# Scatters, staged parts, softmax and the output weight's pieces at new places in a hand-ordered attention step

## The chip, the cores and the metric

The kernel runs on one core of one Trainium2 chip. The metric is device microseconds of one execution. Engines are named as the profile names them: PE is TensorE (matmuls), DVE is VectorE, ACT is ScalarE, POOL is GpSimd, SP is SyncE, which here only issues DMAs.

## The reference, cut to what matters

x is 8 x 2048 x 512 in float32 (8 batches). Six modulation rows per batch (`sa, ca, ga, sb, cb, gb`) come from a small matmul.

```
h = layernorm(x) * (1 + ca) + sa
xn = layernorm(h) * gamma + beta
k, v, r = xn @ Wk.T, xn @ Wv.T, xn @ Wr.T
csum = cumsum(k * v * sigmoid(td) ** t) over the 2048 tokens
wkv = sigmoid(tf) * k * v + sigmoid(td) * (csum shifted by one token)
x = x + ga * ((sigmoid(r) * wkv) @ Wo.T)
h = layernorm(x) * (1 + cb) + sb
x = x + gb * (moe_0(h) + moe_1(h)) / 2     # each: 32 experts, top 2 of a softmax, SwiGLU, 512-256-512
```

## The kernel before, in words

There are two stages. The first, which the change touches, does everything up to the second norm, the router and the lists of tokens for each expert; the second works through the experts' tiles of 128 tokens. Matmuls are made in three passes of float32r: every operand is kept as a high part (a cast, made by ACT) and a low part (the difference, made by POOL or DVE).

The first stage is 32 **steps**, 4 for each batch, of 512 tokens. Batch 0 is written out, batches 1 to 7 are a hardware loop whose body is four steps (s = 0 to 3). Each engine's program has a function `step(b, s, first)` in which its work stands in a fixed order written by hand; semaphores tie the engines together. Work of several steps is in flight: in step s, PE projects step s (`project`, four chunks of 128 output channels, each k, v and r), multiplies Wo for step s-1 (`output`, between chunks 0 and 1), counts ranks for step s-2, transposes the second norm's result of step s-1 (`back`, inside chunk 3), transposes the first norm's result of step s+1 (`front`), and makes the router's logits of step s-1 (`logits`, last).

The names that the text uses:

- DVE: `chunk(dc)` (L829 to L844) turns k, v into the weighted cumulative sum in `cs` (the scan, L841) and `aa`. `topk` (from L894), `place` (L923 to L942, which ends with the scatter indices `sidx`), `residual` (L852, L856), `modulate` (L872, L877, which makes `h2`), and four parts of `norm_front`: statistics of x two steps ahead (part 0, L778), `hb` (part 1, L793), `hb` again with the second set of statistics (part 2, L799), and the small `nmg` (part 3, L815). `split_x` (L822) makes the low part of the transposed input.
- ACT: `chunk_k` (L553), `chunk_r` (L559), `hi(dc)` (L565, the high part `sTh`), `soften` (L583, L585: the softmax's exponentials, with a table load before it and another at the next sigmoid), `turned` (L595), `logits` (L602, the copy of the logits to `lgt`), `normed` (L608), `front` (L616).
- POOL: `receive(dc)` (L678, multiplies by the sigmoid), `lo(dc)` (L701, the low part `sTl`), three `rstd` (L672), `scatter` (L711: 16 indirect DMAs per step put token numbers and weights into the experts' lists).
- The **staged parts**. The experts' weights are split into high and low parts on the way: a step has 10 jobs (40 per batch, of which 4 are the pieces of Wo, which are also scaled by `ga` on POOL in `scale_wo`). Job j is: SP loads 256 KB into `sraw[j % 4]` (`stage_in`), ACT casts it to `shigh[j % 2]` (`stage_hi(j)`, L576), POOL or DVE makes the low part in place (`stage_lo(j)`, L693 or L886), SP stores both halves (`stage_out(j)`, L357, 512 KB). So `stage_hi(j)` waits until job j-2 has been stored. `DVE_LOW` says which jobs of a step have their low part on DVE.
- SP's order in a step is ten turns; turn i stores job i-1, then loads job i+2. After turn 4 stands the 1 MB store of x (`store_x1`), after turn 5 the 1 MB store of `h2` (`store_h2`), after turn 0 the 1 MB load of x. Even turns up to 6 also issue a 256 KB store of a modulation row.

PSUM's 8 banks are handed round: group q of step s lies in bank (26 s + q) mod 8, and PE waits for the reader of the group 8 earlier. So `back` waits for the scan of chunk 1, and the second of `front`'s four groups waits for the scan of chunk 3 (both L841).

## Time and profile before

| | |
|---|---|
| time before, median of 3 runs | 5015.96 us (5013.2 to 5016.27) |
| time of the profiled execution | 5032.62 us, span 5030.9 us |
| PE, DVE, ACT, POOL busy | 92%, 60%, 33%, 56% of the span |
| first stage, steps | from about 80 us to about 2010 us |
| second stage, expert tiles | from about 2120 us to the end |

Busy shares are of the whole span. PE's busy time counts overlapped matmuls and is no measure of how fast it runs; the granted clock (1.00 is 2.4 GHz, 0.50 is 1.2 GHz) stands beside it in the tables of stretches.

### The profile page before, as it was taken

Reading aid. Unit: us, or ns where it says so; the run is one execution under the profiler, and the core shown is the slowest. Engines: PE = TensorE matmul, PEld = TensorE weight load, DVE = VectorE, ACT = ScalarE, POOL = GpSimd, SP = SyncE. Lnnn points to the kernel's source line nnn. Section 1 sums busy time; section 2 is a strip of 40 time slices with the busy share of each in tenths; the row PEclk is TensorE's granted clock in tenths of the full one; section 3 lists DMA queues with packets and bytes.
Section 4 is the critical chain, followed back from the end, with each engine's and each line's share of the span. In section 5 each row is a group of like instructions: output and inputs, shape, how many; then the busy total and the mean of one; then the engine's idle time right before and its main releaser. Section 6 shows DMA issues by size and latency. Waiting matters only on the chain.

```text
span 5030.9 us, 89180 instructions
## 1 busy us (share of the span) xinstructions
PE 4643.5 (92%) x22649; PEld 3825.1 (76%) x22649; DVE 3011.9 (60%) x6077; ACT 1635.8 (33%) x4093; POOL 2804.4 (56%) x2303
## 2 busy tenths in 40 slices
PE   6999999989988999499989998999999999999998
PEld 4777777777777777377777776888788888888886
DVE  5888888888888888444444443554344444444443
ACT  2344444444444444122222222332222222222222
POOL 2576666666666666544454544555455555555554
PEclk8999999999999999799999999999999999999999
DMA  6666565656665656589999989999999989998897
GB/s 234 214 198 212 181 199 181 207 185 213 186 208 185 207 183 199 204 248 277 274 276 268 272 265 271 266 278 248 282 237 245 236 230 253 241 240 215 220 230 192
DMA packets 434624, 1152.46 MB, mean 229 GB/s; under 512 B 59361, under 2 KB 59362, under 8 KB 415666
## 3 DMA queue, kind: packets, MB, share of 16 engines
q0 software_dynamic: 182512, 454.27, 38.8%
q1 hardware_dynamic: 231106, 619.79, 36.2%
q10 hardware_dynamic: 20736, 75.51, 4.0%
q8 instruction: 83, 1.36, 0.1%
q14 instruction: 187, 1.53, 0.1%
HBM read 719.35 MB, written 463.57 MB: 235 GB/s over the span
## 4 chain that ended last, share of the span: by engine, by line
PE 39%; DMA 13%; issue 4%; POOL 2%; DVE 1%; POOLq 0%; SPq 0%; DVEq 0%; ACT 0%
DMA out<-c_yo,c_idx 12%; PE ps L1322 11%; PE ps L1324 11%; PE ps L1323 11%; PE ps L1331 4%; PE ps L1350 2%; DMA c_wt<-wsp_d 1%; POOL out L1313 1%; POOL c_xg L1280 1%; POOLq L1305 0%; DVE c_yo L1577 0%; POOL list_d L1285 0%; DMA list_d<-pairs,sidx 0%; DMA c_lists<-list_d,c_rowu 0%; DVE c_xl L1565 0%
## 5 line engine op out<-in xcount | busy, mean ns | idle before, releaser
L1313 POOL DMA_INDIRECT out<-c_yo,c_idx x576 | 919.0, 1595 | 922.0 <-DMA out<-c_yo,c_idx 481.4
L1322 PE MATMUL ps<-c_wt,c_xh 128*128 128x512 f32 x2304 | 964.7, 419 | 27.6 <-issue 20.3
L1324 PE MATMUL ps<-c_wt,c_xl 128*128 128x512 f32 x2304 | 911.0, 395 | 0.0
L1323 PE MATMUL ps<-c_wt,c_xh 128*128 128x512 f32 x2304 | 904.9, 393 | 0.0
L1280 POOL DMA_INDIRECT c_xg<-h2g_d,c_idx x576 | 566.9, 984 | 512.2 <-DVE c_yo L1577 406.8
L1561 DVE TENSOR_TENSOR c_hh<-ps,c_sil 128x256 f32<-128x256 f32 x576 | 244.1, 424 | 926.1 <-ACT c_sil L1404 926.0
L1577 DVE SCALAR_TENSOR_TENSOR c_yo<-ps,c_wc,c_xg 128x512 f32<-128x512 f32 x576 | 432.4, 751 | 521.2 <-PE ps L1324 265.9
L444 PE MATMUL ps<-xTh,wTh 128*128 128x512 f32 x1536 | 640.1, 417 | 46.9 <-DVE cs L841 34.8
L1409 ACT CAST c_xh<-ps 128x512 fp32r<-128x512 f32 x576 | 337.1, 585 | 957.5 <-PE ps L1331 956.1
L445 PE MATMUL ps<-xTl,wTh 128*128 128x512 f32 x1536 | 627.0, 408 | 0.0
L446 PE MATMUL ps<-xTh,wTl 128*128 128x512 f32 x1536 | 625.4, 407 | 0.0
L711 POOL DMA_INDIRECT list_d<-pairs,sidx x496 | 523.6, 1056 | 177.2 <-issue 120.8
L1404 ACT ACTIVATE c_sil<-ps 128x256 f32<-128x256 f32 x576 | 221.2, 384 | 1181.5 <-PE ps L1324 1181.5
L1322 PE MATMUL ps<-c_wt,c_hTh 128*128 128x512 f32 x1152 | 456.9, 397 | 71.3 <-DVE c_hTl L1570 71.3
L1322 PEld LDWEIGHTS ps<-c_wt,c_xh 128*128 128x128 f32 x2304 | 437.1, 190 | 104.7 <-issue 30.8
L1324 PEld LDWEIGHTS ps<-c_wt,c_xl 128*128 128x128 f32 x2304 | 435.6, 189 | 105.1
L1323 PEld LDWEIGHTS ps<-c_wt,c_xh 128*128 128x128 f32 x2304 | 439.2, 191 | 77.9
L1565 DVE TENSOR_TENSOR c_xl<-ps,c_xh 128x512 fp32r<-128x512 f32 x576 | 397.4, 690 | 132.6 <-ACT c_xh L1409 132.1
L1324 PE MATMUL ps<-c_wt,c_hTl 128*128 128x512 f32 x1152 | 454.9, 395 | 0.0
L1323 PE MATMUL ps<-c_wt,c_hTh 128*128 128x512 f32 x1152 | 452.9, 393 | 0.0
L444 PEld LDWEIGHTS ps<-xTh,wTh 128*128 128x128 f32 x1536 | 307.8, 200 | 125.0 <-DVE cs L841 47.9
L446 PEld LDWEIGHTS ps<-xTh,wTl 128*128 128x128 f32 x1536 | 305.7, 199 | 67.9
(202 smaller groups left out, 7767.7 us busy)
## 6 DMA issues: line engine op xcount, KB each, us to landing
c_wt<-wsp_d SPq DMA_DIRECT2D x69, 2048.0 KB, 11.4
sraw<-wex SPq DMA_DIRECT2D x290, 256.0 KB, 3.5
wsp_d<-shigh SPq DMA_DIRECT2D x288, 256.0 KB
wsp_d<-sraw SPq DMA_DIRECT2D x288, 256.0 KB
c_wt<-wsp_d SPq DMA_DIRECT2D x69, 1024.0 KB, 12.5
xin<-x SPq DMA_DIRECT2D x34, 1024.0 KB, 7.9
h2g_d<-mod_d SPq DMA_DIRECT2D x128, 256.0 KB, 6.2
out<-xin SPq DMA_DIRECT2D x32, 1024.0 KB, 6.7
```

The costliest lines, as they stand in the source:

```text
L444: nc.tensor.matmul(o, lh, rh, start=first, stop=False)
L445: nc.tensor.matmul(o, lh, rl, start=False, stop=False)
L446: return nc.tensor.matmul(o, ll, rh, start=False, stop=last)
L711: nc.gpsimd.indirect_dma_start(out=list_d, out_offset=bass.IndirectOffsetOnAxis(ap=sidx[:, s % 2, i:i + 1], axis=0), in_=pairs[:, s % 2, i ...
L1280: nc.gpsimd.indirect_dma_start(out=xg[:, n % RING, :], out_offset=None, in_=h2g_d, in_offset=bass.IndirectOffsetOnAxis(ap=idx[:, n:n + 1], ...
L1313: nc.gpsimd.indirect_dma_start(out=out, out_offset=bass.IndirectOffsetOnAxis(ap=idx[:, n:n + 1], axis=0), in_=yo[:, n % 4, :], in_offset=N ...
L1322: nc.tensor.matmul(o, lh, rh, start=first, stop=False)
L1323: nc.tensor.matmul(o, lh, rl, start=False, stop=False)
L1324: return nc.tensor.matmul(o, ll, rh, start=False, stop=last)
L1409: nc.scalar.copy(xh[:, s % 2].rearrange("p k t -> p (k t)"), ps[:, 4 + s % 2, :]).then_inc(x_hi, 1)
L1565: V.tensor_tensor(xl[:, s % 2].rearrange("p k t -> p (k t)"), ps[:, 4 + s % 2, :], xh[:, s % 2].rearrange("p k t -> p (k t)").bitcast(F32) ...
L1577: V.scalar_tensor_tensor(out=yo[:, s % 4, :], in0=ps[:, 6 + s % 2, :], scalar=wc[:, s % 4:s % 4 + 1], in1=xg[:, s % RING, C:2 * C], op0=AL ...
```

## The change

The change touches only the first stage. The same instructions are issued in another order, and nothing is left out.

- Wo's pieces are jobs 5 to 8 of a batch in place of 2 to 5; `scale_wo` stands in POOL's step by name.
- The low parts on DVE are jobs 1, 5 and 8 of each step in place of 4, 5 and 6; POOL has 0, 2, 3, 4, 6, 7 and 9.
- ACT: the cast of the next step's job 0 stands at the end of a step, ahead of the copy of the logits; `soften` stands ahead of `chunk_r(0)`; `hi(0)` behind the casts of jobs 2 and 3; the casts of jobs 7 and 8 ahead of `chunk_k(3)`.
- POOL: three scatters stand first in the step, three more after job 0, eight after the third `rstd` as before; `lo(0)` is later; jobs 6 and 7 stand between the eight scatters and `receive(1)`.
- DVE: `topk` is first in the step; job 1's low part follows chunk 0; between `modulate` and chunk 1 only job 5's low part is left; job 8's low part stands between chunk 2 and the statistics of `norm_front` part 0, which stay ahead of chunk 3.
- SP's wait in `stage_out` becomes a `gate` (the same wait, with one for the value 1 ahead of it when the count is in a register).

```diff
-DVE_LOW = (4, 5, 6)
-WO_PART = {2: 0, 3: 1, 4: 2, 5: 3}
+DVE_LOW = (1, 5, 8)
+WO_PART = {5: 0, 6: 1, 7: 2, 8: 3}
...
             def stage_out(b, j):
-                wait(sp, low_of(j), lows(b, j))
+                gate(sp, (low_of(j), lows(b, j)))
...
             def step(b, s, first):          # ACT
-                stage_hi(b, at)
+                if first and s == 0:
+                    stage_hi(b, 0)
                 stage_hi(b, at + 1)
                 chunk_k(b, s, 0)
-                chunk_r(b, s, 0)
-                hi(b, s, 0)
                 if not (first and s < 2):
                     soften(b, s - 2)
+                chunk_r(b, s, 0)
...
             def step(b, s, first):          # DVE
+                if not (first and s < 2):
+                    topk(b, s - 2)
                 norm_front(b, s + 1, 1)
                 chunk(b, s, 0)
-                if not (first and s < 2):
-                    topk(b, s - 2)
+                stage_lo(b, s * PER_STEP + 1)
                 norm_front(b, s + 1, 2)
...
                     place(b, s - 2)
-                stage_lo(b, s * PER_STEP + 4)
                 if not (first and s == 0):
                     modulate(b, s - 1)
                 stage_lo(b, s * PER_STEP + 5)
-                stage_lo(b, s * PER_STEP + 6)
                 chunk(b, s, 1)
                 chunk(b, s, 2)
+                stage_lo(b, s * PER_STEP + 8)
                 norm_front(b, s + 2, 0)
                 chunk(b, s, 3)
```

What now stands where, on two engines. POOL in step 3 of batch 0, from the third `rstd` (`rsb`) on; `sg` is `receive`, `sTl` is `lo`, `sraw<-sraw,shigh` is a job's low part. Before:

```order
L672 TENSOR_TENSOR rsb<-vab,half 128x4
L711 DMA list_d<-pairs,sidx 1048704x2 x8
L678 TENSOR_TENSOR sg<-sg,aa 128x512
L711 DMA list_d<-pairs,sidx 1048704x2
L701 TENSOR_TENSOR sTl<-sg,sTh 128x512
L678 TENSOR_TENSOR sg<-sg,aa 128x512
L693 TENSOR_TENSOR sraw<-sraw,shigh 128x512
```

POOL at the same place of the changed kernel:

```order
L676 TENSOR_TENSOR rsb<-vab,half 128x4
L712 DMA list_d<-pairs,sidx 1048704x2 x8
L697 TENSOR_TENSOR sraw<-sraw,shigh 128x512 x2
L682 TENSOR_TENSOR sg<-sg,aa 128x512
L712 DMA list_d<-pairs,sidx 1048704x2
L702 TENSOR_TENSOR sTl<-sg,sTh 128x512
L682 TENSOR_TENSOR sg<-sg,aa 128x512
```

The low parts of jobs 6 and 7 have moved in between the eight scatters and the multiplication of chunk 1.

ACT in step 3 of batch 0, from `chunk_k(1)` (the first `aa`) on; `sg` is `chunk_r`, `sTh` is `hi`, `h2T` is `turned`, `shigh<-sraw` a job's cast. Before:

```order
L553 ACTIVATE aa<-ps,bias 128x512
L576 CAST shigh<-sraw 128x512
L559 ACT_TABLE_LOAD
L559 ACTIVATE sg<-ps,bias 128x512
L553 ACTIVATE aa<-ps,bias 128x512
L565 CAST sTh<-sg 128x512
L595 COPY h2T<-ps 128x512 x4
L559 ACTIVATE sg<-ps,bias 128x512
L553 ACTIVATE aa<-ps,bias 128x512
L565 CAST sTh<-sg 128x512
L576 CAST shigh<-sraw 128x512 x2
```

ACT at the same place of the changed kernel:

```order
L553 ACTIVATE aa<-ps,bias 128x512
L559 ACTIVATE sg<-ps,bias 128x512
L576 CAST shigh<-sraw 128x512
L553 ACTIVATE aa<-ps,bias 128x512
L576 CAST shigh<-sraw 128x512
L559 ACTIVATE sg<-ps,bias 128x512
L565 CAST sTh<-sg 128x512
L576 CAST shigh<-sraw 128x512
L553 ACTIVATE aa<-ps,bias 128x512
L595 COPY h2T<-ps 128x512 x4
L565 CAST sTh<-sg 128x512
```

The casts of jobs 7 and 8 now stand ahead of the third and fourth `chunk_k` and around `hi(1)`; they stood behind both.

## Rows read from the trace of the kernel before

**Rows 1.** The table of stretches: 29 whole steps of the first stage

The columns are the stretch, its length, then busy time and (count) of PE, PE's weight loads, DVE, ACT, POOL, then PE's granted clock, the DMA share and GB/s.

```profile
187.68:1955.61 1767.93, 1614.04 (x7833) 1334.11 (x7832) 1485.33 (x3248) 735.03 (x1565) 1174.19 (x1008) 0.92 0.63 196
```

**Rows 2.** The waits, 300 to 1900 us: total us, times, longest us

```profile
PE ps L466 <- DVE cs L841: 104.6, 26, 5.3
...
DVE sraw L886 <- ACT shigh L576: 56.0, 19, 3.9
DVE ps L829 <- PE ps L446: 53.4, 25, 6.1
...
DVE nmg L815 <- POOL rsg L672: 46.3, 24, 3.8
```

**Rows 3.** The timeline of PE: start us, duration us, what, [idle before <-releaser]

```profile
187.68 0.48 PE L444 MATMUL ps<-xTh,wTh 128*128 128x512 f32 x1
...
1143.28 2.82 PE L466 MATMUL ps<-ident,h 128*128 128x128 f32 x12 [4.03 <-DVE cs L841]
...
1156.33 3.68 PE L476 MATMUL ps<-rws,h2T 128*128 128x64 f32 x32
...
1955.61 0.48 PE L444 MATMUL ps<-xTh,wTh 128*128 128x512 f32 x1
```

**Rows 4.** The table of stretches: PE's granted clock after two of its waits

```profile
1147.00:1151.00 4.00, 4.00 (x10) 3.13 (x11) 3.39 (x10) 3.12 (x6) 2.11 (x2) 0.50 0.30 84
...
1022.00:1026.00 4.00, 3.82 (x17) 3.17 (x18) 3.93 (x12) 3.11 (x7) 2.48 (x2) 1.00 0.53 140
```

**Rows 5.** The timeline of DVE in one step, and its statistics and scan in another

```profile
1108.27 0.76 DVE L829 SCALAR_TENSOR_TENSOR ps<-ps,bias,aa 128x512 f32<-128x512 f32 x1 [1.88 <-ACT aa L553]
...
1111.85 0.83 DVE L894 MAX8 m<-lgt 128x8 f32<-128x32 f32 x8
...
1115.59 2.73 DVE L799 SCALAR_TENSOR_TENSOR hb<-hb,rsf,mod 128x512 f32<-128x512 f32 x4
...
1121.10 0.68 DVE L852 TENSOR_TENSOR xin<-ps,xin 128x512 f32<-128x512 f32 x1
...
1126.86 1.23 DVE L815 SCALAR_TENSOR_TENSOR nmg<-mvg,rsg 128x4 f32<-128x4 f32 x1
...
1130.52 0.68 DVE L886 TENSOR_TENSOR sraw<-sraw,shigh 128x512 fp32r<-128x512 f32 x1
1131.12 2.73 DVE L872 SCALAR_TENSOR_TENSOR h<-xin,mvb,mod 128x512 f32<-128x512 f32 x4
...
1022.83 2.46 DVE L778 BATCH_NORM_STATS2 stf<-xin 128x6 f32<-128x512 f32 x4
...
1027.29 1.28 DVE L841 TENSOR_TENSOR_SCAN cs<-ones,cs,ps 128x512 f32<-128x512 f32 x1
```

**Rows 6.** The timeline of DVE and POOL at the start of a step

```profile
1158.67 6.13 DVE L793 SCALAR_TENSOR_TENSOR hb<-xin,mvf,mod 128x512 f32<-128x512 f32 x4
...
1161.02 3.24 POOL L693 TENSOR_TENSOR sraw<-sraw,shigh 128x512 fp32r<-128x512 f32 x2 [0.17 <-ACT shigh L576]
```

**Rows 7.** The timeline of SP: issues of the h2 store and of job 9's load

```profile
1136.73 0.39 SPq L331 DMA_DIRECT2D h2g_d<-h  x1
...
1147.47 0.36 SPq L370 DMA_DIRECT2D sraw<-wex  x1
```

**Rows 8.** The timeline of POOL: first of eight scatters, then receive(1)

```profile
1131.37 1.41 POOL L711 DMA_INDIRECT list_d<-pairs,sidx  x1 [2.34 <-DVE sidx L942]
...
1144.10 1.27 POOL L678 TENSOR_TENSOR sg<-sg,aa 128x512 f32<-128x512 f32 x1 [2.37 <-DVE aa L844]
```

**Rows 9.** The timeline of ACT: soften behind hi(0), and the copy of the logits

```profile
1119.33 0.62 ACT L565 CAST sTh<-sg 128x512 fp32r<-128x512 f32 x1 [10.60 <-PE ps L446]
1119.97 1.28 ACT L583 ACT_TABLE_LOAD   x1
...
1123.82 1.13 ACT L576 CAST shigh<-sraw 128x512 fp32r<-128x512 f32 x2
...
1160.05 0.37 ACT L602 COPY lgt<-ps 128x256 f32<-128x256 f32 x1 [1.03 <-PE ps L476]
```

More of the change, by code:

```diff
@@ L633, in step @@
                 chunk_k(b, s, 1)
+                chunk_r(b, s, 1)
                 stage_hi(b, at + 6)
-                chunk_r(b, s, 1)
                 chunk_k(b, s, 2)
+                stage_hi(b, at + 7)
+                chunk_r(b, s, 2)
                 hi(b, s, 1)
+                stage_hi(b, at + 8)
+                chunk_k(b, s, 3)
                 if back_too:
                     turned(b, s)
-                chunk_r(b, s, 2)
-                chunk_k(b, s, 3)
                 hi(b, s, 2)
-                stage_hi(b, at + 7)
-                stage_hi(b, at + 8)
-                front(b, s, (0, 1))
+                stage_hi(b, at + 9)
                 chunk_r(b, s, 3)
-                front(b, s, (2, 3))
+                front(b, s, range(KC))
                 hi(b, s, 3)
+                if s < 3:
+                    stage_hi(b, at + 10)
+                else:
+                    stage_hi(b + 1, 0)
                 if back_too:
                     logits(b, s)
-                stage_hi(b, at + 9)
             normed(0, -1)
@@ L693, in stage_lo @@
                 nc.gpsimd.tensor_tensor(dst, sraw[:, j % 4], high.bitcast(F32), ALU.subtract).then_inc(low_pool, 1)
-                for i in (j + 1,) if j < 3 else (j + 1, j + 2):
-                    if i in WO_PART:
-                        scale_wo(b, i)
             def lo(b, s, dc):
@@ L716, in step @@
                 old = not (first and s < 2)
+                older = not (first and s < 3)
                 at = s * PER_STEP
+                if older:
+                    scatter(b, s - 3, 10, 13)
+                rstd(f_var, vaf, h_ready, rsf, f_rstd, b, s + 1)
                 stage_lo(b, at)
-                if not (first and s < 3):
-                    scatter(b, s - 3, 11, 13)
-                rstd(f_var, vaf, h_ready, rsf, f_rstd, b, s + 1)
-                stage_lo(b, at + 1)
+                if older:
+                    scatter(b, s - 3, 13, 16)
                 receive(b, s, 0)
-                if not (first and s < 3):
-                    scatter(b, s - 3, 13, 14)
-                lo(b, s, 0)
-                if not (first and s < 3):
-                    scatter(b, s - 3, 14, 16)
                 stage_lo(b, at + 2)
@@ L731, in step @@
                 stage_lo(b, at + 3)
+                lo(b, s, 0)
+                stage_lo(b, at + 4)
                 if not (first and s == 0):
                     rstd(b_var, vab, h2_ready, rsb, b_rstd, b, s - 1)
+                if s == 0:
+                    scale_wo(b, 5)
+                    scale_wo(b, 6)
                 if old:
                     scatter(b, s - 2, 0, 8)
+                if s == 0:
+                    scale_wo(b, 7)
+                stage_lo(b, at + 6)
+                if s == 0:
+                    scale_wo(b, 8)
+                stage_lo(b, at + 7)
                 receive(b, s, 1)
@@ L792, in norm_front @@
                     for j in range(TJ):
[L793 to L794 removed]
+                        V.scalar_tensor_tensor(out=hb[:, j, :], in0=xin[:, u, j, :],
+                                               scalar=mvf[:, j, 0:1], in1=mod[:, CA1, :],
+                                               op0=ALU.subtract, op1=ALU.mult).then_inc(h_half, 1)
                 elif part == 2:
```

19 lines of the change are left out of this document (7 added, 12 removed).

## The prediction

> **What bounds the kernel now.** I read the table of stretches first. Over 29 whole steps of the first stage [rows 1] PE's granted clock is 0.92, DVE is busy for 1485.33 of 1767.93 us, and 1767.93 / 29 = 60.96 us is the length of a step. DVE's own work is 1485.33 / 29 = 51.2 us of it. The second stage is untouched, so all that can change is the 60.96, some 30 times (32 steps, of which the first two have no scatters).
>
> The waits come next [rows 2]. In each of 26 steps PE stands 104.6 / 26 = 4.0 us ahead of `back` until DVE has made the scan of chunk 1. DVE is late there because of its own waits: 56.0 / 26 = 2.2 us a step for the cast of a staged part (job 6), ahead of chunk 1; 1.8 us for `rstd`, ahead of `nmg`; and 2.1 us for PE, which had been late from its own stall. So a loop from DVE to PE and back sets the step, and a stall of PE costs more than its length: after the 4.03 us wait at 1143 us [rows 3] the stretch 1147 to 1151 us still runs at 0.50, the 1.2 GHz level [rows 4]; after another wait of such length the second of these stretches is already at 1.00, 2.4 GHz. What follows the wait (12 transposes in 2.82 us [rows 3]) runs at the low level.
>
> The timeline of DVE gives the price of each piece, taken from start to start [rows 5]: chunk 0 3.58 us, `topk` 3.74, `norm_front` part 2 5.51, `residual` 5.76, `nmg` with `place` 3.66 (of which 1.23 is `nmg`, four elements a lane, so mostly a wait in disguise), one low part 0.60, the four instructions of half of `modulate` 2.73; from the statistics of part 0 to the end of the next scan 1027.29 + 1.28 - 1022.83 = 5.74.
>
> **What the change removes.** `topk` moves into the time in which DVE waited for chunk 0 (1.88 us in [rows 5]). Job 6's low part and its 2.2 us of waiting leave the place ahead of chunk 1, and job 4's leaves too; job 1's low part comes in. `soften` used to stand behind `hi(0)`, which waits 10.60 us for the end of `output` [rows 9]; behind it came the casts and low part that POOL's `rstd` for `nmg` was queued behind. From its table load to the next cast it is 1123.82 - 1119.97 = 3.85 us of ACT, now spent while PE runs chunk 0 and the Wo matmuls, so I cost it at nothing: its cover is the ten us and more until `residual`. By DVE's pieces the scan of chunk 1 now ends at about 36 us after the logits, before PE reaches `back`; the stall of 4.0 us there goes. `scale_wo` and SP's extra wait for 1 add instructions of no length that matters beside waits.
>
> **What is late next.** The price is on ACT, POOL and SP. On ACT the cast of job 8 now stands behind the cast of job 7 and behind `hi(1)`; DVE's low part of job 8 waits for it, and behind it are queued the statistics and chunk 3, whose scan releases `front` on PE. On POOL the low parts of jobs 6 and 7 stand ahead of `receive(1)`, on which `hi(1)` waits. And the cast of job 7 waits until job 5 has been stored, which SP issues behind the 1 MB store of `h2`. I work this loop out from the end of PE's logits (time 0):
>
> - logits copied 0.4 [rows 9], `topk` from 0.5 to 4.2, `norm_front` part 1 to 7.2 (2.73 plus 0.3), chunk 0 to 10.8, job 1's low part 11.4
> - `norm_front` part 2: 5.51, plus 1.5 for a clash with POOL (below), to 18.4; `residual` to 24.2; `nmg` and `place` 3.2 (3.66 less half of what `nmg` waited) to 27.4
> - `modulate` up to SP's issue of the `h2` store: 1136.73 - 1131.12 = 5.6 us [rows 5, 7], at 33.0
> - job 5 stored: before, SP's load of job 9, which waits for just that, came 1147.47 - 1136.73 = 10.7 us after the `h2` store [rows 7]. Then job 6's store and a store of x shortly ahead shared the DMA engines; now job 6's store comes later and the store of x, due at the end of `residual` (24.2), has 9 us to drain. I take 7.5 (choice, between 5.4, where POOL would be last, and 10.7), at 40.5
> - cast of job 7 0.7 (half of 1.13 for two [rows 9], and a hand-over), low part 7 on POOL 1.4, `receive(1)` 1.3 (1.27 [rows 8]), `hi(1)` 0.7, cast of job 8 0.5, low part 8 on DVE 0.7 plus 0.3: at 46.1
> - statistics and chunk 3 up to its scan 5.74, at 51.9
> - PE has then stood some 5 us, so the 12 remaining transposes of `front` take 2.8 and the logits 3.68 plus 1.0 (between 0, if the clock is back, and 3, if it is not): 59.5
>
> POOL's own path is shorter: eight scatters from the end of `place` take 1144.10 - 2.37 - 1131.37 = 10.4 us [rows 8], and the low part of job 6 ends at 39.1, ahead of job 7's cast. In the steps with Wo's pieces two scalings of 1.3 us stand on this path, but no store is waited for, and the end is within 1 us of the same. What each engine loses at the loop's edge fell on DVE's path; now DVE waits for the logits in that time. I leave this gain out as a margin.
>
> The sum: 60.96 - 59.5 = 1.5 us a step, times 30 is 44 us. The profiled execution took 5032.62 us with a span of 5030.9, 17 us above the median of 5015.96; the difference is taken off the median: 4972 us.
>
> **The clash with POOL.** Four instructions of L793 took 6.13 us [rows 6] where four of the same shape took 2.73 [rows 5], and POOL's two low parts beside them took 3.24 us, not two times 1.27. Both sides read only SBUF. Before, part 2 of `norm_front` met no POOL arithmetic; now `receive(0)` and job 2's low part fall beside it, two instructions of 1.3 us, so the bounds are 0 and 2.6, and with the larger share falling on DVE I take 1.5. Part 1 instead meets mainly scatters, and gains what L793 lost. The Trainium skill says in SBUF — State Buffer, section Who interferes with whom, that a VectorE instruction with two SBUF inputs contends with a GpSimd instruction that reads SBUF, and that the later one blocks fully. By that rule, the trace agrees at L793, and the clash would come at the upper bound of 2.6; by the rows alone 1.5 stands.
>
> **The rivals.**
>
> *The stall moves and grows (slower).* If job 5's store takes the old 10.7 us after the `h2` store, all behind it is 3.2 later: 62.7 us a step, 1.8 more than before, 53 us: 5069. It decides at 9.0 us: below that the kernel is faster, above it slower. For it: the only row that shows this store is 10.7. Against it: less is in flight. Chance 0.28.
>
> *POOL and DVE alone set the pace (much faster).* The store is done by the time low part 6 ends (5.4 us), which saves 2.1, the clock is back for the logits, 1.0, and the clash of 1.5 is small: 56.4 us a step or less, 137 us: about 4880. Against it: 1.75 MB have to go through in 5.4 us. Chance 0.17.
>
> *The stall only changes place (no change).* PE's 4 us ahead of `back` become 5 us ahead of the second group of `front`, and the low clock falls on the logits, which are now waited for by `topk`: with 1.5 more for the clock the step is 61.0 us: 5016. Chance 0.10.
>
> *The clash is full and also hits low part 8 (slightly slower).* 1.1 more in part 2, 0.9 more at job 8 and 0.5 in `place`: 62.0, 5047. Chance 0.05.
>
> **How the numbers follow.** The forecast, 4972 (its own range 4945 to 5000, which is 0.9 us a step either way), has 0.40. The two slower cases give 0.33, the one of no change 0.10, the faster ones 0.57. A difference under 0.2%, 10 us, can't be told from no change. The range goes from 4890, near the much faster case, to 5070, the old time of the store; outside lie its combination with a full clash or a low clock through the whole of the logits (5100 and more), and the very short step.
>
> **What would show it.** Right: in the waits PE's 104.6 us ahead of L466 nearly gone, and a new wait of 4 to 7 us a step ahead of `front` for the scan; DVE waiting for the cast of job 8 for some 4 us; L793 near 0.8 us in the mean, four of L799 above the 2.73 us of [rows 5]; DVE idle ahead of `topk` until the logits are copied; ACT waiting for a store ahead of job 7's cast. Job 7's cast beginning 7.5 us after the `h2` store would confirm the term on which the sign hangs; 10 us would prove me wrong, and so would a step whose length is set by some queue that I took for covered, such as `rstd` for the second norm behind `lo(0)` and job 4's low part.

## The result

The changed kernel is slower: 5164.22 us in the median (5147.25 to 5171.11, 4 runs) beside 5016.11 for the kernel before (5013.2 to 5043.67, 4 runs), a ratio of 1.0273 (95% interval 1.0239 to 1.0306). I had forecast 4972 with a range from 4890 to 5070; sign and range were both wrong. The profiled execution of the changed kernel has a span of 5167.2 us.

To compare steps I read in the timeline of PE the start of `logits` in one step and in the step 27 later. Before, these lie at 360.99 and 2015.88 us, a mean step of 61.29 us; after, at 370.22 and 2139.79, a mean of 65.54. That is 4.25 us more a step. Over the whole profiled executions the spans differ by 5167.2 - 5030.9 = 136.3 us. The second stage begins at 2069.45 us before and at 2197.33 us after, so 127.9 us of this lie in the first stage. The other 8.5 (2961.4 us of second stage before, 2969.9 after) are no more than this untouched stage varies by: over all profiles of this study it takes 2952 to 2972 us. The table of stretches over these 27 steps of the changed kernel (columns as in [rows 1]):

```profile
370.22:2139.79 1769.57, 1541.05 (x7291) 1303.83 (x7291) 1396.61 (x3024) 691.23 (x1458) 1116.77 (x943) 0.87 0.57 183
```

DVE is busy 1396.61 / 27 = 51.7 us a step, beside 51.2 before [rows 1]; the granted clock fell from 0.92 to 0.87. More waiting, not more work. The waits of the changed kernel, 300 to 1900 us (total us, times, longest):

```profile
ACT shigh L576 <- DMA wsp_d<-sraw: 275.6, 57, 10.8
PE ps L487 <- DVE cs L847: 205.3, 25, 10.3
...
DVE m L900 <- ACT lgt L602: 132.4, 25, 5.9
DVE sraw L892 <- ACT shigh L576: 115.9, 18, 8.3
...
ACT woh L576 <- POOL sraw L689: 56.9, 6, 11.2
```

PE's wait ahead of `back` [rows 2] is gone, as forecast. In its place PE waits ahead of the second group of `front`, for the scan of chunk 3 (L847): 205.3 / 25 = 8.2 us each time, twice what was removed. DVE waits 115.9 / 18 = 6.4 us for ACT's cast of job 8, and ACT waits for stores: ahead of job 7's cast, 9.6 us in the mean of the steps without Wo's pieces. In the kernel before, that cast never waited. In one step of four, where jobs 5 to 8 are Wo's pieces, ACT waits for POOL's scaling instead (56.9 / 6 = 9.5 us). The timeline of PE in two steps that follow each other, which answers to [rows 3]:

```profile
1217.75 2.82 PE L487 MATMUL ps<-ident,hb 128*128 128x128 f32 x12 [7.13 <-DVE cs L847]
1220.36 6.93 PE L476 MATMUL ps<-rws,h2T 128*128 128x64 f32 x32
...
1282.88 2.82 PE L487 MATMUL ps<-ident,hb 128*128 128x128 f32 x12 [7.38 <-DVE cs L847]
1285.49 6.93 PE L476 MATMUL ps<-rws,h2T 128*128 128x64 f32 x32
```

The logits take 6.93 us here where they took 3.68 [rows 3]; in 22 of the 27 steps they take over 6.9. The table of stretches inside the second of these shows a granted clock of 0.50, the 1.2 GHz level:

```profile
1286.00:1289.00 3.00, 3.00 (x16) 3.00 (x16) 0.89 (x2) 1.36 (x3) 2.12 (x3) 0.50 0.57 192
```

Between these two logits I can follow the chain of my prediction. The timeline of DVE, ACT, SP and POOL (start, duration, what):

```profile
1227.79 0.85 DVE L900 MAX8 m<-lgt 128x8 f32<-128x32 f32 x8 [5.87 <-ACT lgt L602]
...
1238.42 1.33 POOL L682 TENSOR_TENSOR sg<-sg,aa 128x512 f32<-128x512 f32 x1 [4.78 <-ACT sg L559]
1239.72 1.75 POOL L697 TENSOR_TENSOR sraw<-sraw,shigh 128x512 fp32r<-128x512 f32 x1
...
1238.53 4.81 DVE L805 SCALAR_TENSOR_TENSOR hb<-hb,rsf,mod 128x512 f32<-128x512 f32 x4
...
1260.42 0.39 SPq L331 DMA_DIRECT2D h2g_d<-h  x1
...
1262.04 1.12 SPq L357 DMA_DIRECT2D wsp_d<-shigh  x1
1263.37 0.41 SPq L357 DMA_DIRECT2D wsp_d<-sraw  x1
...
1269.67 0.62 ACT L576 CAST shigh<-sraw 128x512 fp32r<-128x512 f32 x1 [9.26 <-DMA wsp_d<-sraw]
1270.20 0.68 ACT L559 ACTIVATE sg<-ps,bias 128x512 f32<-128x512 f32 x1
1272.93 0.62 ACT L565 CAST sTh<-sg 128x512 fp32r<-128x512 f32 x1 [2.05 <-POOL sg L682]
1273.46 0.61 ACT L576 CAST shigh<-sraw 128x512 fp32r<-128x512 f32 x1
1273.98 0.68 ACT L553 ACTIVATE aa<-ps,bias 128x512 f32<-128x512 f32 x1
...
1271.61 1.29 POOL L682 TENSOR_TENSOR sg<-sg,aa 128x512 f32<-128x512 f32 x1
1273.05 1.00 POOL L712 DMA_INDIRECT list_d<-pairs,sidx  x1 [0.15 <-issue]
1274.09 1.30 POOL L702 TENSOR_TENSOR sTl<-sg,sTh 128x512 fp32r<-128x512 f32 x1
1275.34 1.26 POOL L682 TENSOR_TENSOR sg<-sg,aa 128x512 f32<-128x512 f32 x1
...
1274.11 3.05 DVE L892 TENSOR_TENSOR sraw<-sraw,shigh 128x512 fp32r<-128x512 f32 x1 [6.17 <-ACT shigh L576]
1277.08 2.46 DVE L783 BATCH_NORM_STATS2 stf<-xin 128x6 f32<-128x512 f32 x4
...
1281.54 1.28 DVE L847 TENSOR_TENSOR_SCAN cs<-ones,cs,ps 128x512 f32<-128x512 f32 x1
```

What to see: SP issues the store of `h2` 33.1 us after the end of the logits (1220.36 + 6.93 = 1227.3), and my chain said 33.0. From there it goes wrong. Job 7's cast starts 1269.67 - 1260.42 = 9.25 us after that store is issued and has waited 9.26 us. All that the step still has to do before `front` is queued behind it on ACT: the sigmoid of chunk 2, `hi(1)`, job 8's cast, chunk 3's k. DVE's low part of job 8 waits for its cast and then takes 3.05 us instead of 0.68. Neither is peculiar to this step: of the 27 steps 26 have this low part at 3.02 to 3.06 us, and in the 21 whose job 7 is no piece of Wo the cast comes 9.4 us after the store in the mean. Chunk 3's scan ends at 1282.8, 55.5 us after the logits, where I had 51.9.

### The profile page after: what moved, and what is told of

Its sections match the earlier page's. It is cut to its first block, busy times and chain, and to the rows that moved or that the text cites. A ratio compares the mean times of both kernels' runs of the same rounds, so it can differ in the third digit from the quotient of the medians.

```text
span 5167.2 us, 89483 instructions
## 1 busy us (share of the span) xinstructions
PE 4684.2 (91%) x22649; PEld 3889.8 (75%) x22649; DVE 3027.1 (59%) x6077; ACT 1643.6 (32%) x4094; POOL 2826.4 (55%) x2303
## 4 chain that ended last, share of the span: by engine, by line
PE 41%; DMA 11%; issue 3%; POOL 1%; DVE 1%; POOLq 0%; SPq 0%; DVEq 0%; ACT 0%
PE ps L1328 12%; PE ps L1330 12%; PE ps L1329 12%; DMA out<-c_yo,c_idx 10%; PE ps L1337 4%; PE ps L1356 2%; POOL out L1319 0%; POOL c_xg L1286 0%; DMA c_wt<-wsp_d 0%; DVE c_yo L1583 0%; POOL list_d L1291 0%; POOLq L1311 0%; DMA list_d<-pairs,sidx 0%; DVE c_xl L1571 0%; DMA c_lists<-list_d,c_rowu 0%
## 5 line engine op out<-in xcount | busy, mean ns | idle before, releaser
L712 POOL DMA_INDIRECT list_d<-pairs,sidx x496 | 540.1, 1089 | 194.4 <-issue 128.5
L444 PE MATMUL ps<-xTh,wTh 128*128 128x512 f32 x1536 | 624.3, 406 | 17.5 <-DVE cs L847 8.8
L445 PE MATMUL ps<-xTl,wTh 128*128 128x512 f32 x1536 | 613.0, 399 | 0.0
L446 PE MATMUL ps<-xTh,wTl 128*128 128x512 f32 x1536 | 611.1, 398 | 0.0
L487 PE MATMUL ps<-ident,hb 128*128 128x128 f32 x528 | 110.5, 381 | 276.4 <-DVE cs L847 250.5
```

What stands on the lines that cost most here:

```text
L444: nc.tensor.matmul(o, lh, rh, start=first, stop=False)
L445: nc.tensor.matmul(o, lh, rl, start=False, stop=False)
L446: return nc.tensor.matmul(o, ll, rh, start=False, stop=last)
L712: nc.gpsimd.indirect_dma_start(out=list_d, out_offset=bass.IndirectOffsetOnAxis(ap=sidx[:, s % 2, i:i + 1], axis=0), in_=pairs[:, s % 2, i ...
```

## The experiments

The time is set against runs of the kernel before on the same chip; the step is the mean over 27 steps, read as above.

| kernel | median us | ratio to before (95%) | step us | logits over 5 us long |
|---|---|---|---|---|
| before | 5016 to 5038 | 1 | 61.29 | 0 of 27 |
| changed | 5164.22 | 1.0273 (1.0239 to 1.0306) | 65.54 | 22 |
| changed, low part 8 behind chunk 3 | 5008.43 | 0.9944 (0.9924 to 0.9965) | 60.12 | 8 |
| changed, `h2` store behind job 5's | 5092.44 | 1.0114 (1.0071 to 1.0158) | 63.09 | 7 |
| changed, top-2 put back | 5166.67 | 1.0261 (1.0217 to 1.0305) | 65.05 | 9 |
| before, top-2 first | 5022.32 | 0.9985 (0.9967 to 1.0004) | 60.56 | 0 |
| changed, receive ahead of low part 7 | 5102.61 | 1.0125 (1.0108 to 1.0142) | 63.71 | 17 |
| changed, second half put back ("back") | 4994.42 | 0.9911 (0.9895 to 0.9928) | 59.55 | 8 |
| changed, logits first | 5068.23 | 1.0062 (1.0045 to 1.0078) | 62.13 | 27 |
| back, logits first | 4940.76 | 0.9804 (0.9788 to 0.9820) | 57.99 | 2 |
| changed, wait filled | 5126.71 | 1.0195 (1.0168 to 1.0221) | 64.20 | 11 |
| changed, low part 8 one column | 5155.01 | 1.0254 (1.0230 to 1.0278) | 65.37 | 21 |
| back, logits first, `h2` store later | 4932.24 | 0.9829 (0.9797 to 0.9860) | 58.00 | 4 |
| before, casts 7 and 8 early | 5140.19 | 1.0231 (1.0204 to 1.0257) | 64.72 | 9 |
| before, logits first | 5034.61 | 1.0002 (0.9986 to 1.0018) | 60.94 | 0 |
| back, logits first, cast 9 late | 4882.34 | 0.9696 (0.9671 to 0.9721) | 55.95 | 3 |
| the same, chunk 3's k earlier | 4901.47 | 0.9727 (0.9700 to 0.9754) | 56.88 | 6 |
| changed, chunk 3's k ahead of casts | 4893.97 | 0.9724 (0.9697 to 0.9751) | 56.58 | 5 |

### One thing at a time out of the changed kernel

**Low part 8 behind chunk 3**, on DVE:

```diff
-                stage_lo(b, s * PER_STEP + 8)
                 norm_front(b, s + 2, 0)
                 chunk(b, s, 3)
+                stage_lo(b, s * PER_STEP + 8)
```

> The changed kernel, with job 8's low part on VectorE behind chunk 3 in place of ahead of the statistics. My theory: VectorE's wait for the cast of job 8 (6.2 us in the step from 1227 us) and that low part's 3.05 us stand in the loop that sets the step; without them chunk 3 waits only for its chunk_k, so its scan ends 5.2 us sooner, and if TensorE's shorter wait lets the clock be back for the logits, up to 3.3 us more come: 5.2 to 8.5 us a step, 155 to 255 us, so 4910 to 5010. Rival (the two buffers of the staged parts set the pace, and VectorE only shows it): job 8 is stored later, the casts behind it come later too, under 1 us a step, 5135 to 5165. Rival (the early topk sets the pace, by its wait for the logits): nothing changes either.

It is 0.56% faster than before and takes 3.2% off the changed kernel, by moving one instruction that takes 0.68 us alone. The step is 65.54 - 60.12 = 5.4 us shorter, at the lower end of my theory's 5.2 to 8.5. PE's wait ahead of `front` halves, from 205.3 us in 25 times to 107.6 in 26. The timeline of DVE in this kernel:

```profile
1238.76 2.46 DVE L783 BATCH_NORM_STATS2 stf<-xin 128x6 f32<-128x512 f32 x4
...
1247.79 0.76 DVE L835 SCALAR_TENSOR_TENSOR ps<-ps,bias,aa 128x512 f32<-128x512 f32 x1 [6.09 <-ACT aa L553]
...
1251.35 3.70 DVE L892 TENSOR_TENSOR sraw<-sraw,shigh 128x512 fp32r<-128x512 f32 x1
```

The wait has not gone: DVE now waits 6.09 us for chunk 3's k, which is behind the same casts on ACT. But the statistics run inside the wait, and the low part stands behind chunk 3. It is no shorter there (3.70 us); it is only that chunk 3 no longer stands behind it.

**The same low part, one column wide**, in its place (the rest of these low parts is left out):

```diff
+                n = 1 if j % PER_STEP == 8 and j not in WO_PART else C
-                V.tensor_tensor(dst, sraw[:, j % 4], high.bitcast(F32), ALU.subtract)
+                V.tensor_tensor(dst[:, 0:n], sraw[:, j % 4, 0:n], high[:, 0:n].bitcast(F32), ALU.subtract)
```

> The changed kernel with DVE's low part of job 8 cut to one column of its 512 where the job is a part of the weights' split (left out of the computation: the rest of these low parts, so that their stored halves are raw). Its place, and its wait for ACT's cast of job 8, stay. It tells the duration (3.05 us at its place between GpSimd's operations; 0.68 where nothing ran beside it) from the wait (5.8 to 6.2 us). Theory by the rows: some 2.8 us less in each of 27 of 31 steps, and less where the front wait then ends at something else: 60 to 80 us, so 5090 to 5110 us. Rival A (the wait is all, GpSimd's operation only gets its share of the port sooner, and chunk 3's first operation meets it in its place): 5140 to 5170. Rival B (moving the low part behind chunk 3, which gave 5008, gained by the duration alone): below 5050.

Almost nothing, as rival A has it, but not for its reason. The timeline of DVE and POOL shows that a single column took 2.53 us:

```profile
1217.64 2.53 DVE L893 TENSOR_TENSOR sraw<-sraw,shigh 128x1 fp32r<-128x1 f32 x1 [6.05 <-ACT shigh L576]
...
1217.62 1.31 POOL L702 TENSOR_TENSOR sTl<-sg,sTh 128x512 fp32r<-128x512 f32 x1
1218.87 1.27 POOL L682 TENSOR_TENSOR sg<-sg,aa 128x512 f32<-128x512 f32 x1
```

It starts 0.02 us behind the first of two POOL instructions and ends 0.03 us after the second (1220.17 and 1220.14). All 19 such instructions from 300 to 2000 us took 2.48 to 2.53 us. So the 3.05 us of this low part were no slower work; DVE stood until POOL had done both. What can be gained there is the place, not the size.

**The store of `h2` behind the turn of job 6**, that is behind job 5's store, on SP:

```diff
                 turn(5)
+                turn(6)
                 if not (first and s == 0):
                     store_h2(b, s - 1)
...
-                for i in range(6, PER_STEP):
+                for i in range(7, PER_STEP):
```

> The changed kernel, with SP's 1 MB store of h2 behind turn 6, so that job 5 is stored ahead of it. My theory: job 7's cast, which came 9.3 us after the store of h2 was issued, comes some 4 us sooner, and its low part, receive(1), hi(1) and the cast of job 8 follow until POOL's own path (low part 6 ends at 1268.0) or job 6's store holds them: 0 to 2.3 us a step, 0 to 70 us, so 5095 to 5165; above all the 9.3 us must shrink in the trace. Rival (the h2 store is not what job 5's store waits for, the engines are simply full): the cast of job 7 comes as late as before, 5164.

1.5% better than the changed kernel, and with 5092.44 us just below the 5095 to 5165 of my theory. In its timeline job 7's cast starts 3.9 us after job 5's store is issued, where the changed kernel needed 7.6 (1262.04 to 1269.67); the wait is 5.30 us and no longer 9.26:

```profile
1223.01 0.34 SPq L357 DMA_DIRECT2D wsp_d<-shigh  x1
...
1226.87 0.62 ACT L577 CAST shigh<-sraw 128x512 fp32r<-128x512 f32 x1 [5.30 <-DMA wsp_d<-sraw]
```

So the store of `h2` ahead of it is worth some 4 us of that wait (3.7 in the mean of the steps without Wo's pieces, from 9.6 to 5.9). The step got 2.4 shorter in the mean over all steps; where job 7 is a piece of Wo, its cast waits for no store.

**GpSimd's receive of chunk 1 ahead of the low part of job 7:**

```diff
-                stage_lo(b, at + 7)
                 receive(b, s, 1)
+                stage_lo(b, at + 7)
```

> The changed kernel with one move on GpSimd: the receive of chunk 1 (L682, L697) stands ahead of the low part of job 7, which takes 1.24 us, and no longer behind it. In the trace of the changed kernel job 7's cast ends at 1270.4, receive 1 starts at 1271.6 and hi(1) at 1272.9. My theory: the receive waited for nothing but GpSimd, hi(1) starts up to 1.2 us earlier, the cast of job 8 (1273.5) follows if job 6's store has landed, and job 8's low part, chunk 3 and the front wait move with it: 0.5 to 1.2 us in each of some 30 steps, 15 to 36 us, so 5125 to 5150 us. Rival A: job 8's cast waits for job 6's store and nothing moves: 5155 to 5170. Rival B: the earlier receive falls on a DVE operation and stretches it: 5170 to 5190.

1.4% better than the changed kernel, more than I had worked out (5102.61 us, where the theory had 5125 to 5150): 1.8 us a step for an instruction of 1.24 us. The rest, 0.6 us, is what the logits got shorter in the mean (6.47 to 5.88 us); they were long in 17 steps and no longer in 22. DVE's waits ahead of job 8's low part fell from 115.9 to 57.9 + 33.3 = 91.2 us in all (the second part without a releaser).

**The top-2 put back** behind chunk 0 (DVE), and `soften` behind chunk 0's sigmoid (ACT):

```diff
-                if not (first and s < 2):
-                    topk(b, s - 2)
                 norm_front(b, s + 1, 1)
                 chunk(b, s, 0)
+                if not (first and s < 2):
+                    topk(b, s - 2)
```

> The changed kernel, with topk back behind chunk 0 and soften behind chunk_r(0). My theory: chunk 0 already starts when TensorE releases it (it waited 0.2 us for TensorE), so topk's 3.7 us come on top, and all behind it is later by that: 112 us slower, about 5275, with VectorE idle ahead of chunk 0. Rival (topk's wait for the logits at 1.2 GHz, 5.9 us a step, is what made the change slower): taking topk off that place gives back 2 us a step or more, 5100 or below.

Neither: no change. The top-2 should add 3.7 us to the chain. Against it stand two gains that the trace shows: `norm_front` part 2 meets no POOL instruction and takes 2.73 us again instead of 4.81, and the logits were long in 9 steps instead of 22. That these are the whole of what cancels the 3.7 us is worked out, not tested.

**The same move made in the kernel before:**

> The kernel before, with only this of the change: topk first in VectorE's step, and soften ahead of chunk_r(0) on ScalarE. My theory: place ends 3 us sooner, the low part and the cast of jobs 4 and 6 follow it, TensorE's 4.0 us ahead of the back transposes shrink to about 1, and the step is 2.5 to 4 us shorter: 75 to 120 us, 4895 to 4940. Rival (the early topk is the harm in the change, since it waits for the logits): 5016 or slower, with a new wait of 2 us or more ahead of MAX8.

No change either; the rival had it, time and new wait both: DVE waits 43.1 us in 21 times ahead of MAX8 for the copy of the logits. And its `nmg` now waits 82.9 us in all for POOL's `rstd`, beside 46.3 [rows 2]: POOL has it behind the low part of job 2 and `lo(0)`. What the early top-2 could gain, these two waits take up.

### How much is the clock

**The wait filled**: 56 transposes of the identity ahead of `front`, overwritten by the real ones:

```diff
                     bank_free(pe, b, s, FRONTT + k)
+                    if k == 0 and fill:
+                        for i in range(56):
+                            nc.tensor.transpose(bank(s, FRONTT)[:, 0:P], ident[:], ident[:])
```

> The changed kernel, and ahead of each step's 16 front transposes 56 transposes of the identity into the bank of the first of them, whose results are overwritten: work of 0.12 us each at the full clock, 6.7 us in all, laid into TensorE's wait of 7 to 9 us for chunk 3. It tells what the fall of the granted clock costs. In the changed kernel the logits behind that wait took 6.29 us in the mean over the steps (3.68 at the full clock) and the 12 transposes 2.82 (1.5 in steps at the full clock). Theory (the clock is a term of the step of its own, some 2.5 to 4 us of the excess over before): logits 3.7, transposes 1.5, the wait for chunk 3 as before less the filling: 2.5 to 4 us in each of some 30 steps, 5050 to 5095 us. Rival A (the clock is a symptom: what it costs is given back by stores that then come no earlier): logits 3.7 but 5130 to 5170. Rival B: the filling itself outlasts the wait in many steps: above 5170.

0.8% better than the changed kernel, between theory and rival A. The 56 transposes ran at the full clock (granted clock 1.00 from 1202.6 to 1208.6 us). The timeline of PE in this kernel shows why not more:

```profile
1202.51 6.28 PE L488 MATMUL ps<-ident 128*128 128x128 f32 x56
1208.62 0.60 PE L490 MATMUL ps<-ident,hb 128*128 128x128 f32 x4
1211.36 1.68 PE L490 MATMUL ps<-ident,hb 128*128 128x128 f32 x12 [2.14 <-DVE cs L850]
1212.84 6.93 PE L476 MATMUL ps<-rws,h2T 128*128 128x64 f32 x32
```

Even after a wait of only 2.14 us the logits ran at the low level in this step, as in 11 of 27; in the step after it, with a wait of 1.84 us, they took 3.68. The mean of the logits went from 6.47 to 5.13 us, which is 1.34 us a step, and the step from 65.54 to 64.20, the same 1.34. The equality may be chance, since the 12 transposes got shorter too (1.68 us here, 2.82 in the changed kernel). But the filling changes nothing except what PE does in its wait, so the clock is a term of its own: this part of it is 1.34 of the 4.25 us by which the change lengthened the step. What the clock costs in full stays open, because the filling left it low in 11 steps.

**The logits ahead of `front`** on PE, and their copy ahead of the front's on ACT:

```diff
-                front(b, s)
                 if not (first and s == 0):
                     logits(b, s)
+                front(b, s)
```

> The changed kernel with TensorE's logits ahead of the 14 front transposes of the next step, ACT's copy of the logits ahead of the copies of the front. In the changed kernel TensorE waits 7.4 us for chunk 3 before the front transposes and then runs the logits in 6.9 us at half the clock; the logits need nothing that chunk 3 makes. My theory: the logits then run in the wait for chunk 3 and leave the loop, the step loses most of the 6.9 us less what transposes at the half clock add: 4 to 6.5 us in each of some 30 steps, so 4970 to 5045 us. Rival A: the loop is set by DVE and the store of h2, whose top-2 start earlier but whose later steps wait for the same stores (job 7's cast at 9.25 us behind the store): 5100 to 5165. Rival B: the transposes of the back, on which the logits wait, end so late that the logits now hold up the front: 5170 to 5250.

3.4 us a step, short of the theory's 4 to 6.5 (the transposes of `front` are 16, and not 14). The logits no longer stand behind chunk 3, but they wait for h2T, which ACT copies behind job 8's cast, and all 27 are long:

```profile
1223.77 7.06 PE L476 MATMUL ps<-rws,h2T 128*128 128x64 f32 x32 [3.58 <-ACT h2T L595]
```

**The same in the kernel before:**

> The kernel before with TensorE's logits ahead of the 16 front transposes, and on ACT the sigmoid of chunk 3 and the copy of the logits ahead of the copies of the front. It tells whether that edit, which took 50 to 55 us off the kernel with the second half put back, is worth something without the early statistics. Theory: in the kernel before, the loop goes from the logits over DVE's top-2 and the norms to the back transposes (back wait of 4.1 us in the mean); logits that start 1.9 us earlier (16 transposes) bring all of it forward: 1 to 1.9 us in each of 30 steps, 4960 to 4995 us. Rival: the top-2 stand behind chunk 0 on DVE, and chunk 0 waits for the front's halves, which now come 3.7 us later; the loop is unchanged or longer: 5010 to 5100 us.

Nothing: 5034.61 us, in the rival's range and not in my theory's. There the logits ran at the full clock in either place (0 of 27 long), and to bring them forward alone brings nothing.

### The order of the casts

**The second half put back**: behind chunk 1's sigmoid the order of before on ACT up to job 8's cast (job 9's stays where the change has it), with low part 7 on POOL and low part 8 on DVE later to match:

```diff
                 stage_hi(b, at + 6)
                 chunk_k(b, s, 2)
-                stage_hi(b, at + 7)
-                chunk_r(b, s, 2)
                 hi(b, s, 1)
-                stage_hi(b, at + 8)
-                chunk_k(b, s, 3)
                 if back_too:
                     turned(b, s)
+                chunk_r(b, s, 2)
+                chunk_k(b, s, 3)
                 hi(b, s, 2)
+                stage_hi(b, at + 7)
+                stage_hi(b, at + 8)
                 stage_hi(b, at + 9)
```

> The changed kernel with its first half of the step kept (norm and statistics early on DVE, top-2 first, stores as changed), but the second half in the order of before: casts of jobs 7 and 8 on ACT behind hi(2), the low part of job 7 on GpSimd behind receive 1, the low part of job 8 on DVE behind chunk 3. My theory: the cast of job 7, which in the changed kernel waits 9.3 us for the store of h2, then stands on nobody's way, chunk 3 follows chunk 2 as soon as its inputs are in PSUM, the front wait of 7.4 us before the transposes goes and little of the back wait of 4.1 us of before comes back: 4860 to 4960, faster than both kernels (at 4980 or above this falls). Rival A (GpSimd's queue): the scatters and low parts that come behind let receive 1 or the gate arrive late, and the time is that of before, 5000 to 5040. Rival B (the late casts push the following job's store and the next half's cast of job 1 or 2 late): 5060 to 5160.

0.9% faster than before, which by my own bound (4980) is not the theory; it lies just below rival A. The rest of the change thus helps, and what made the whole of it slow lies in the second half.

**The casts of jobs 7 and 8 early in the kernel before**, and of the rest of the change only what goes with them on POOL: job 7's low part ahead of `receive(1)`, job 8's ahead of `lo(2)`. On ACT:

```diff
+                stage_hi(b, at + 7)
                 hi(b, s, 1)
                 if back_too:
                     turned(b, s)
                 chunk_r(b, s, 2)
+                stage_hi(b, at + 8)
                 chunk_k(b, s, 3)
```

> The kernel before with its first half of the step as it was, and only the casts of jobs 7 and 8 on ACT, with job 7's low part on GpSimd, moved ahead as in the change: cast 7 ahead of hi(1), cast 8 ahead of chunk 3's k. It tells whether the early casts are harmful by themselves. Theory: cast 7 waits for the store two jobs back, which stands behind SP's store of h2; hi(1), the sigmoid of chunk 2 and chunk 3 wait with it, a front wait of 3 to 8 us comes, and the back wait of 4 us stays or shrinks: 5070 to 5200 us. Rival: in the kernel before h2 is stored so late against ACT's order that cast 7's store is long done, and the time stays within 20 us of before.

2.31% slower, of the 2.73% of the whole change. In its timeline job 7's cast starts 9.5 us after the store of `h2`, and `hi(1)` then waits for `receive(1)`, which stands behind job 7's low part on POOL:

```profile
1198.82 0.39 SPq L331 DMA_DIRECT2D h2g_d<-h  x1
...
1208.31 0.62 ACT L576 CAST shigh<-sraw 128x512 fp32r<-128x512 f32 x1 [4.31 <-DMA wsp_d<-sraw]
1211.56 0.62 ACT L565 CAST sTh<-sg 128x512 fp32r<-128x512 f32 x1 [2.64 <-POOL sg L678]
```

Its waits of PE, 300 to 1900 us, have the old wait ahead of `back` in full and a new one ahead of `front`:

```profile
PE ps L466 <- DVE cs L841: 106.4, 25, 6.1
PE ps L487 <- DVE cs L841: 45.9, 25, 3.4
```

The new wait is 45.9 / 25 = 1.8 us each time, less than the 3 to 8 of my theory, though the time lies in its range. The share of job 7's low part in the 2.31% was not taken apart; in the changed kernel its place ahead of `receive(1)` was worth 1.4%.

**Chunk 3's k ahead of the casts**, everything else of the change kept but the low parts that belong to them (job 7's on POOL behind `lo(1)`, job 8's on DVE behind chunk 3):

```diff
-                stage_hi(b, at + 7)
                 chunk_r(b, s, 2)
                 hi(b, s, 1)
-                stage_hi(b, at + 8)
                 chunk_k(b, s, 3)
+                stage_hi(b, at + 7)
+                stage_hi(b, at + 8)
```

> The changed kernel with only this put differently: on ACT the sigmoid of chunk 2, hi(1) and the k of chunk 3 stand ahead of the casts of jobs 7 and 8, GpSimd's low part of job 7 stands behind lo(1), DVE's low part of job 8 behind chunk 3. The copies of h2T, hi(2), the cast of job 9 and the sigmoid of chunk 3 still stand behind the two casts. It tells whether it is enough that nothing of chunk 3's recurrence waits for the two stores. Theory: chunk 3 ends behind chunk 2 and the statistics, the front wait goes, and the casts' wait falls on h2T and the logits instead, which TensorE's front covers in part: the time of the kernel with the second half put back, 4970 to 5030 us. Rival A: h2T and with it the logits come so late that TensorE waits for them and their clock falls: 5060 to 5170. Rival B: with chunk 3 free it beats that kernel: below 4960.

2.8% faster than the kernel before, 5.3% faster than the changed one; rival B, the most favourable of the three. Its waits, and its timeline of ACT and DVE:

```profile
PE ps L487 <- DVE cs L847: 30.4, 23, 5.1
```

```profile
1296.67 0.68 ACT L553 ACTIVATE aa<-ps,bias 128x512 f32<-128x512 f32 x1
1297.25 0.61 ACT L576 CAST shigh<-sraw 128x512 fp32r<-128x512 f32 x1
1299.93 0.62 ACT L576 CAST shigh<-sraw 128x512 fp32r<-128x512 f32 x1 [2.07 <-DMA wsp_d<-sraw]
...
1294.74 2.46 DVE L783 BATCH_NORM_STATS2 stf<-xin 128x6 f32<-128x512 f32 x4
...
1297.62 0.76 DVE L835 SCALAR_TENSOR_TENSOR ps<-ps,bias,aa 128x512 f32<-128x512 f32 x1
```

Chunk 3 follows the statistics without a gap. Job 7's cast, which waited 9.26 us, no longer waits here (0.6 us at most in any of 27 steps), for its store is done by then. Job 8's waits 2.07 us, and chunk 3 is not behind it. PE's wait ahead of `front` is 30.4 us in all and no longer 205.3.

**On top: logits first, later store, later cast 9, earlier k.** The second half put back and the logits first together:

> Both edits at once: second half in the order of before, and logits ahead of the front transposes. My theory: with the casts out of the way chunk 3 ends close behind chunk 2, so the front is ready when the back ends and there is no wait left for the logits to fill; the logits ahead of the front then cost what they take, and the time is that of the second half alone, within 25 us of it either way. Rival: the logits at once behind the back bring DVE's top-2 forward by the 2.8 us of transposes, the whole first half starts that much earlier, and the step loses up to 2.8 us more: 60 to 90 us below the second half alone.

The rival, nearly: 1.07% below the second half alone (0.9804 beside 0.9911), 54 us; the logits' own place pays once the casts are out of their way. With the store of `h2` behind the turn of job 6 as well:

> The first half of the step as changed, the second half in the order of before, the logits ahead of the front transposes (that kernel ran in 4941 us), and SP's store of h2 behind the turn of job 6, as in the run that gained 72 us on the changed kernel. Theory: with the casts of jobs 7 and 8 behind hi(2) no engine waits on their stores early enough for SP's order to matter: within 20 us of 4941, 4920 to 4960. Rival A: job 6's cast still waits for job 5's store behind h2's; freed of it, the step loses 0.5 to 1.5 us more: 4890 to 4925. Rival B: the later store of h2 holds DVE's modulate of the next step, which overwrites h2: above 4970.

No further gain, as the theory has it (0.9829 beside 0.9804). With the cast of job 9 behind the copies of the front on ACT:

> The kernel of second half back and logits first (ratio 0.980 to before), with ACT's cast of job 9 behind the copies of the front instead of ahead of the sigmoid of chunk 3. In that kernel's trace the cast waits 3.95 us for job 7's store, the copies of the front and DVE's low parts of x stand behind it, and TensorE waits 2.2 to 2.7 us in the step for them. Theory: that wait goes, 1.5 to 2.5 us in each of some 30 steps: 4865 to 4900 us. Rival A: the cast of job 9 only moves its wait to hi(3), and TensorE's output waits for that instead: 4915 to 4950. Rival B: the later cast delays job 9's store and with it the casts of jobs 1 and 2 ahead of chunk 0's sigmoid: above 4960.

The theory, and the fastest kernel of the study: 3.04% below before. The step with Wo's pieces gains least: 62.7 us, beside 54.0 for the other three; before, these were 63.3 and 60.7. With chunk 3's k earlier still:

> As the run before, and chunk 3's k on ACT ahead of the copies of h2T and the sigmoid of chunk 2 (2.7 us of ACT). In the trace of the base kernel DVE waits 2.3 us for that k. Theory: chunk 3 ends 2.3 us earlier, but TensorE waits for the front's copies and not for chunk 3, so within 15 us of the run before. Rival A: with the cast of job 9 out of the way chunk 3 is what the front waits for, and the step loses another 0.5 to 2 us: 15 to 60 us below the run before. Rival B: h2T comes 0.7 us later, the logits wait for it: 10 to 30 us above.

Rival B: 0.3% above the run before it (4901.47 beside 4882.34).

## Why the prediction was wrong

**Right.** The stall ahead of `back` went. The chain up to the store of `h2` held: 33.1 us beside 33.0. DVE idles ahead of the top-2, four of the first norm's instructions take 2.73 us, PE waits ahead of `front` for chunk 3, and ACT waits for a store ahead of job 7's cast. The clash in part 2 was 4.81 - 2.73 = 2.08 us, where I took 1.5 between 0 and 2.6.

DVE's idle time ahead of the cast of job 8 and PE's ahead of `front` were both longer than the signs that I had named: 6.4 us where I had some 4, and 8.2 where I had 4 to 7.

**The failed step** is the sum from the store of `h2` to the end of the logits. The prediction has 59.5 - 33.0 = 26.5 us for it; in the step read it was 32.0 (from 1260.42 to 1285.49 + 6.93 = 1292.42). The path was right and three of its terms were too small. The first is "job 5 stored ... I take 7.5", on which I had hung the sign: it was 9.25 up to the start of the cast, 1.75 more. I had named 9.0 as the point from which the kernel is slower, and gave that side 0.28 and a time of 5069. But this term alone makes the step 61.25 us, 0.3 above the 60.96 of before; most of the loss comes from the other two, the cost of low part 8 and the clock in the logits, and they would have turned the sign without it. With the clash ahead of the store these are the terms:

| term | I took | measured | difference |
|---|---|---|---|
| clash in `norm_front` part 2 | 1.5 | 2.1 | +0.6 |
| `h2` store to job 7's cast | 7.5 | 9.25 | +1.75 |
| low part 8 | 1.0 | 3.05 | +2.05 |
| logits behind the wait | 4.7 | 6.93 in 22 of 27 steps (mean 6.47) | +1.8 |

Together 6.2 us; small terms elsewhere came out shorter, and 59.5 became 65.5. The experiments bear on the same three: the place of low part 8 gives back 5.4 us of a step (with the wait that stood ahead of it), the place of the `h2` store 2.4, and the part of the clock that the filling won 1.3. Low part 8 was mis-sized because I took 0.3 us for contact with POOL, as if it were a chance meeting. It is none. When `receive(1)` ends (1271.61 + 1.29 = 1272.90), it sets off two chains of almost the same length. POOL issues one scatter and starts `lo(1)` at 1274.09, right behind it (`hi(1)`, which `lo(1)` needs too, was done at 1273.55); ACT makes `hi(1)` and the cast of job 8, and DVE starts at 1274.11. In 26 of the 27 steps DVE comes 0.01 to 0.03 us behind `lo(1)`. Two events that one event sets off, each a fixed time later, meet in every step.

The Trainium skill says in SBUF — State Buffer, section Who interferes with whom, that the port pair which DVE and GpSimd share is an exclusive lock, so that the later of two contending instructions stands still. The one-column run agrees that DVE stood still: 2.53 us for one column. It stood through two POOL instructions, where the Trainium skill speaks of the one that came first. For the clash in `norm_front` part 2 the prediction works out 2.6 us by the rule of the Trainium skill: of that 2.08 fell on DVE and 1.33 + 1.75 - 2 x 1.27 = 0.54 on POOL.

**What the sum hid.** I treated the store as a length in a chain that could not be otherwise. The runs show that the chain itself was the edit to look at: the early casts with their low parts on POOL cost the kernel before 2.31%, and with the casts behind chunk 3's k and their low parts later the same change gains 2.8%. So the other parts of the change are worth more than the 1.5 us a step that I forecast; the step with chunk 3's k ahead of the casts is 4.7 us shorter than that of before. The forecast of 59.5 was the sum of a large gain and a large loss that I did not price apart.

**Open.** Which of the remaining parts makes the 2.8% is not settled. The early top-2 alone give nothing, and in the changed kernel their loss costs nothing; whether they count once the casts are out of the way was not tried, and neither were the new places of the scatters, of `hi(0)` and of Wo's pieces alone. The low parts of jobs 7 and 8 moved together with the casts, so the casts' own share is not known apart from theirs. Steps with Wo's pieces take 67.3 us in the changed kernel beside 65.0 for the others; I had put this within 1 us, but before it was 63.3 beside 60.7, so the change did not add it. Nor was it tried to make the store of `h2` smaller, so its 4 us are known by its place in SP's queue only.

## What to carry to other kernels

In an engine's queue the place of an operation that waits for a DMA is a property of everything behind it. Put it behind the last operation on which another engine's recurrence hangs: there the 9 us wait of job 7's cast was gone, since its store had had the time, and the 2 us that job 8's still waited held up nothing that set the step. A few places ahead, the same wait made every step longer. Price each order edit alone, also those that only seem to fill a gap, before adding up the chain. And when a wait moves on the matmul engine, look at what stands right behind it, for that is what runs at the low clock.

## What was not expected of the hardware

- A DVE instruction of one column, on two SBUF inputs, took 2.53 us beside two POOL instructions that followed each other without a gap; it was not let in between the two.
- After waits of 8.2 us in the mean the logits took over 6.9 us in 22 of 27 steps, with the granted clock at 0.50 in the stretch shown, after 2.8 us of transposes that ran no faster. In the kernel before, after 4 us of waiting, it was back in time for them in every step [rows 3, 4], with the rest of chunk 3 between. With the wait filled, and 83.0 / 25 = 3.3 us of it left, the logits were still long in 11 of 27 steps.
- A store issued behind the 1 MB store of `h2` released the cast that waits for it 7.6 us after its issue, and 3.9 us after when issued ahead of it (7.8 and 4.2 in the mean of the steps without Wo's pieces).
